# The last cross-attention batch is filled with layer norm and query and key projections of half the tokens

## The reference

```
x = x + cross_attention(layernorm(x), ctx)   # ctx: 16 x 1601 rows of 256; 16 heads of 16
x = x + self_attention(layernorm(x))         # 16 heads of 16, rotary embedding on q and k
x = x + mixture_of_experts(layernorm(x))     # 8 experts, top 2, and a shared part
x = x + linear(layernorm(x)) + mean of the projected context
x = x + self_attention(layernorm(x))         # 8 heads of 64, relative position bias
x = x + grouped_ffn(layernorm(x))
```

## Time and profile before

| | us |
|---|---|
| median of 3 runs | 1324.93 (1324.72 to 1325.19) |
| profiled execution | 1311.63 |
| span of its instructions | 1309.8 |
| TensorE busy in the span | 1186.6 (91%) |
| VectorE busy | 700.4 (53%) |
| ScalarE busy | 563.2 (43%) |
| GpSimd busy | 381.8 (29%) |

### The profile page before, as it was taken

One profiled execution on the slowest core, in us unless ns is written; L12 is line 12 of the kernel. 1 busy time (PEld: TensorE's weight loads), 2 busy tenths in 40 slices (PEclk: granted clock), 3 DMA queues, 4 the chain that ended last, 5 costly groups with the idle time before them and its releaser, 6 DMA issues. The chain is left out here.

```text
span 1309.8 us, 32326 instructions
## 1 busy us (share of the span) xinstructions
PE 1186.6 (91%) x13863; PEld 1043.7 (80%) x13863; DVE 700.4 (53%) x1111; ACT 563.2 (43%) x923; POOL 381.8 (29%) x339
## 2 busy tenths in 40 slices
PE   4799999999999999999999998787798999388799
PEld 4789989989989989989989986676577777266588
DVE  6555655655655655655655633266663221554732
ACT  4465555555555555555555552234631322121500
POOL 5632432432432432432432410044245000422000
PEclk9899999999999999999999995579989999689999
DMA  6937747747747647747647533083012121405054
GB/s 199 212 79 171 160 87 169 161 89 168 166 85 174 158 87 170 161 88 176 157 88 170 120 80 74 1 278 145 2 69 89 49 65 49 124 21 213 2 184 190
DMA packets 61732, 161.47 MB, mean 123 GB/s; under 512 B 24904, under 2 KB 38296, under 8 KB 58520
## 3 DMA queue, kind: packets, MB, share of 16 engines
q1 hardware_dynamic: 58904, 154.18, 46.6%
q0 software_dynamic: 1536, 4.20, 0.9%
q10 hardware_dynamic: 1152, 1.05, 0.2%
HBM read 70.56 MB, written 9.44 MB: 61 GB/s over the span
## 5 line engine op out<-in xcount | busy, mean ns | idle before, releaser
L366 ACT ACTIVATE xa_pt<-xa_sc 128x1024 f32<-128x1024 f32 (+1 forms) x224 | 212.4, 962 | 151.2 <-PE xa_sc L558 151.2
L412 DVE TENSOR_REDUCE xa_mx<-xa_sc 128x2 f32<-128x804 f32 x256 | 243.4, 991 | 41.5 <-PE xa_sc L542 41.5
L558 PE MATMUL xa_sc<-xa_queries,xa_keys 104*128 104x128 f32 (+1 forms) x1664 | 232.5, 285 | 2.6 <-DVE xa_queries L427 1.8
L558 PEld LDWEIGHTS xa_sc<-xa_queries,xa_keys 104*128 104x128 f32 (+1 forms) x1664 | 206.6, 195 | 21.4 <-issue 8.7
L479 PE MATMUL xa_pj<-xa_ctx_hi,xa_wk 128*128 128x400 f32 (+1 forms) x512 | 156.8, 348 | 0.9 <-DVE xa_qst L440 0.9
L479 PE MATMUL xa_pj<-xa_wv,xa_ctx_hi 128*128 128x256 f32 (+1 forms) x832 | 155.3, 286 | 0.1
L542 PE MATMUL xa_sc<-xa_keys,xa_queries 96*128 96x402 f32 x512 | 138.0, 373 | 13.1 <-DMA xa_keys<-xa_kst_hi 7.5
L569 PE MATMUL xa_op<-xa_pt,xa_values 128*32 128x64 f32 x6656 | 141.6, 228 | 7.7 <-ACT xa_pt L366 3.3
L295 POOL TENSOR_TENSOR xa_ctx_lo<-xa_raw,xa_ctx_hi 128x1600 fp32r<-128x1600 f32 (+1 forms) x32 | 115.9, 3624 | 78.0 <-DVE xa_ctx_hi L405 75.4
L300 POOL TENSOR_TENSOR xa_kst_lo<-xa_wk,xa_kst_hi 128x400 fp32r<-128x400 f32 x64 | 67.3, 1051 | 227.5 <-ACT xa_kst_hi L345 227.5
L479 PEld LDWEIGHTS xa_pj<-xa_wv,xa_ctx_hi 128*128 128x128 f32 (+1 forms) x832 | 126.1, 184 | 8.0 <-issue 6.6
(11 more groups left out here) (288 smaller groups left out, 1722.7 us busy)
## 6 DMA issues: line engine op xcount, KB each, us to landing
xa_keys<-xa_kst_hi SPq DMA_DIRECT2D x256, 200.2 KB, 6.1
xa_keys<-xa_kst_lo SPq DMA_DIRECT2D x128, 200.2 KB, 5.3
xa_raw<-in_ctxT SPq DMA_DIRECT2D x15, 1601.0 KB, 9.0
gf_w<-in_gf_w SPq DMA_DIRECT2D x16, 1024.0 KB, 7.1
moe_ex<-in_moe_ex SPq DMA_DIRECT2D x8, 1088.0 KB, 15.3
xa_queries<-xa_qst SPq DMA_DIRECT2D x96, 32.0 KB, 3.5
moe_slots_in<-in_moe_zero SPq DMA_DIRECT2D x1, 2944.0 KB, 16.2
moe_xs<-moe_slots_in SPq DMA_DIRECT2D x23, 128.0 KB, 2.2
```

What stands on the lines that cost most here:

```text
L366: nc.scalar.activation(PT[ptslot(step)][0:rows, 0:nt], SC[bank(step)][0:rows, 0:nt], ACT.Exp, scale=float(D0) ** -0.5).then_inc(ex_done, 1)
L412: nc.vector.tensor_reduce(mx[:, u // 2, 2 * (u % 2):2 * (u % 2) + 2], SC[bank(step)][:, :, 0:MXN], AX.X, ALU.max).then_inc(mx_done, 1)
L558: last = mm(SC[bank(step)][0:rows, kk, a * P:(a + 1) * P], KS[:, 2 * a + h, kt * P:kt * P + rows], QS[b % 2][:, 2 * a + h, :], start=True, ...
```

## The change

Tokens 0 to 511 (four of the eight tiles, `EARLY_TILES`) belong to batches 0 to 7, whose output steps are over long before batch 15. For them the second layer norm and the projections q, qr, k, kr are made inside `xattn`:

- first half of batch 14: "as" takes mean and variance (VectorE), the root (ScalarE), and writes the normalized tiles `ey` into the free context buffer;
- second half of batch 14: four "N" steps, two transposes each on TensorE and a copy to `lnT` on ScalarE; behind the st steps "lh" (two) and "wh" (four) split `lnT` and the weights, high parts on ScalarE, low parts on GpSimd. SyncE loads the four weights into the context buffer as soon as the last context is split;
- batch 15: eight "P" steps, four in each half, three of them between the mx steps and one ahead of mt. Each is 6 matmuls of 512 columns, a copy to SBUF on ScalarE and a multiply with cos or sin on GpSimd, every second one also an add. After each four, SyncE writes a query or key tile to DRAM (512 KB).

Layer norm 1 and the projections of `self_attention` then run over tokens 512 to 1023 alone; the values are made of all tokens. SyncE reads the early tiles back at the start of `self_attention`, ahead of the expert weights, and `projected` waits for them. The new buffers lie in the free parts of existing ones (context, key stage), which brings the waits on `kst_in` and `full["V"]`. The diff, cut to this:

```diff
@@ -35,11 +35,11 @@
-RING = ("K", "V", "Q", "E", "W")
+RING = ("K", "V", "Q", "E", "W", "N", "P")
 SCORES = ("mx", "st")
-def xattn_phase(b, h, fill, chain, late):
+def xattn_phase(b, h, fill, chain, late, between={}):
     out, fill, late = [], list(fill), dict(late)
@@ -47,6 +47,7 @@
         out.append(("mx", b, h, u))
         if fill and (u in (1, 3, 4, 6) or u >= 1 and len(fill) > 4):
             out.append(fill.pop(0))
+        out += between.get(u, [])
     out += fill + chain[:2] + [("mt", b, h, 0)] + chain[2:3]
     for g in range(7):
         out.append(("st", b, h, g))
@@ -67,12 +68,25 @@
     for b in range(B):
         queries = {2: [("Q", b // 2 + 1, 0, 0)]} if b % 2 and b + 1 < B else {}
         e = [("E", b - 1, 0, 0)] if b else []
+        if b == B - 1:
+            project = [("P", 0, 0, m) for m in range(len(EARLY))]
+            half = len(project) // 2
+            o += xattn_phase(b, 0, project[:half - 1], project[half - 1:half], {1: e})
+            o += xattn_phase(b, 1, project[half:-1], project[-1:], {})
+            continue
+        between, split_early = [{}, {}], {}
+        if b == B - 2:
+            between = [{2: [("as", 0, 0, 0)], 5: [("as", 0, 0, 1)]}, {u: [("N", n, 0, 0)] for n, u in enumerate((0, 2, 5, 7))}]
+            split_early = {1 + n: [("lh", 0, 0, n)] for n in range(CH)} | {3 + n: [("wh", 0, 0, n)] for n in range(4)}
         w = [("W", b // 2 - 1, 0, u) for u in range(2)] if b and b % 2 == 0 else []
-        o += xattn_phase(b, 0, K(b + 1, 0), V(b + 1, 0, 4), {1: e} | queries)
-        o += xattn_phase(b, 1, K(b + 1, 1) + w, V(b + 1, 4, 7), {1: split(b + 2)[:1], 4: split(b + 2)[1:]})
+        o += xattn_phase(b, 0, K(b + 1, 0), V(b + 1, 0, 4), {1: e} | queries, between[0])
+        o += xattn_phase(b, 1, K(b + 1, 1) + w, V(b + 1, 4, 7), {1: split(b + 2)[:1], 4: split(b + 2)[1:]} | split_early, between[1])
     return o + [("E", B - 1, 0, 0)] + [("W", T - 1, 0, u) for u in range(2)]
+EARLY_NAMES = ("q", "qr", "k", "kr")
+EARLY = [(n + r, ch) for n in "qk" for ch in range(CH) for r in ("", "r")]
+EARLY_TILES = T // 2
 KCOLS = [(0, 400), (400, 800), (800, 1200), (1200, NKP)]
...
@@ -253,6 +283,16 @@
                         sp.wait_ge(rows_in, 16)
                         for a in range(4):
                             sp.dma_start(*constant_rows(o_sb, slice(96 + 2 * a, 98 + 2 * a), 2 * a, 2 * a + 2)).then_inc(rows_in, 16)
+                if step == ("cv", B - 1, 0, 1):
+                    sp.wait_ge(csum_done, nth(*step) * 2)
+                    sp.wait_ge(lo_done, nth(*step))
+                    for n in EARLY_NAMES:
+                        sp.dma_start(split_by_ch(ew_raw[n]), w["sa_" + n]).then_inc(ew_in, 16)
+                if k == "P" and u in (len(EARLY) // 2 - 1, len(EARLY) - 1):
+                    j = u // (len(EARLY) // 2)
+                    sp.wait_ge(e_rot, (j + 1) * CH)
+                    sp.dma_start(early_out[j], early[j]).then_inc(early_done, 16)
                 if step in (("K", 0, 0, 3), ("K", 0, 1, 3)):
                     keys(0, h)
...
@@ -299,6 +339,28 @@
                     pool.wait_ge(khi, nth(*step))
                     nc.gpsimd.tensor_tensor(kstage[h][1][:, lo:hi], kraw[u % 2][:, 0:hi - lo],
                                             kstage[h][0][:, lo:hi].bitcast(f32), ALU.subtract).then_inc(klo, 1)
+                if k == "wh":
+                    pool.wait_ge(ewh_done, u + 1)
+                    n = EARLY_NAMES[u]
+                    nc.gpsimd.tensor_tensor(ew_lo[n], split_by_ch(ew_raw[n]), ew_hi[n].bitcast(f32), ALU.subtract).then_inc(ewl_done, 1)
+                if k == "lh":
+                    pool.wait_ge(elh_done, u + 1)
+                    nc.gpsimd.tensor_tensor(el_lo[:, u], lnT[:, u, 0:wide], el_hi[:, u].bitcast(f32), ALU.subtract).then_inc(ell_done, 1)
+                if k == "P":
+                    name, ch = EARLY[u]
+                    dst, turned = early["qk".index(name[0])][:, ch, :], name[1:] != ""
+                    by_batch = lambda a: a.rearrange("p (b s) -> p b s", s=S)
+                    table = c["sin" if turned else "cos"].unsqueeze(1).to_broadcast([P, wide // S, S])
+                    pool.wait_ge(free["P"], nth(*step))
+                    if turned:
+                        ge(pool, e_rot, u // 2)
+                    nc.gpsimd.tensor_tensor(by_batch(erot if turned else dst), by_batch(estage[u % 2]), table, ALU.mult).then_inc(e_mul, 1)
+                    if turned:
+                        pool.wait_ge(e_mul, nth(*step))
+                        nc.gpsimd.tensor_tensor(dst, dst, erot, ALU.add).then_inc(e_rot, 1)
                 if k == "E":
                     pool.wait_ge(rec_done, nth(*step))
...
@@ -357,6 +419,31 @@
                     for kk in range(nt):
                         ins = nc.scalar.activation(vdst[:, kk], vsrc[:, kk], ACT.Copy)
                     ins.then_inc(free["V"], 1)
+                elif step == ("as", 0, 0, 0):
+                    act.wait_ge(e_var, 1)
+                    nc.scalar.activation(estd[:], evar[:], ACT.Sqrt).then_inc(e_std, 1)
+                elif k == "N":
+                    act.wait_ge(full["N"], nth(*step))
+                    nc.scalar.activation(lnT[:, :, b * P:(b + 1) * P], PJ[bank(step)][:, 0:D].rearrange("p (c n) -> p c n", c=CH),
+                                         ACT.Copy).then_inc(free["N"], 1)
+                elif k == "wh":
+                    act.wait_ge(ew_in, 16 * len(EARLY_NAMES))
+                    act.wait_ge(kst_in[0], 16 * DMAS_K * B)
+                    n = EARLY_NAMES[u]
+                    nc.scalar.activation(ew_hi[n], split_by_ch(ew_raw[n]), ACT.Copy).then_inc(ewh_done, 1)
+                elif k == "lh":
+                    act.wait_ge(full["V"], nth("V", B - 1, 0, 6))
+                    act.wait_ge(free["N"], EARLY_TILES)
+                    nc.scalar.activation(el_hi[:, u], lnT[:, u, 0:wide], ACT.Copy).then_inc(elh_done, 1)
+                elif k == "P":
+                    act.wait_ge(full["P"], nth(*step))
+                    if u == 0:
+                        act.wait_ge(full["V"], nth("V", B - 1, 0, 6))
+                    ge(act, e_mul, u - 1)
+                    nc.scalar.activation(estage[u % 2], PJ[bank(step)][:, 0:wide], ACT.Copy).then_inc(free["P"], 1)
                 elif k == "st":
...
@@ -452,6 +539,20 @@
                         dve.wait_ge(free["W"], nth(*step))
                         nc.vector.bn_stats(stats[:, b], X[:, b]).then_inc(stats_done, 1)
+                elif step == ("as", 0, 0, 0):
+                    dve.wait_ge(stats_done, EARLY_TILES)
+                    for t in range(EARLY_TILES):
+                        nc.vector.bn_aggr(emv[:, t], stats[:, t]).then_inc(e_stat, 1)
+                    dve.wait_ge(e_stat, EARLY_TILES)
+                    nc.vector.tensor_scalar(evar[:], emv[:, :, 1], 1e-5, None, ALU.add).then_inc(e_var, 1)
+                elif step == ("as", 0, 0, 1):
+                    dve.wait_ge(e_std, 1)
+                    nc.vector.reciprocal(erstd[:], estd[:]).then_inc(e_stat, 1)
+                    dve.wait_ge(e_stat, EARLY_TILES + 1)
+                    dve.wait_ge(lo_done, nth("cv", B - 1, 0, 1))
+                    for t in range(EARLY_TILES):
+                        nc.vector.tensor_scalar(ey[t], X[:, t], emv[:, t, 0:1], erstd[:, t:t + 1], ALU.subtract, ALU.mult).then_inc(e_norm, 1)
                 elif k == "pv" and u == 6:
                     dve.wait_ge(pv_done, nth(*step))
...
@@ -522,6 +623,18 @@
                             last = mm(dst[:, half * P:(half + 1) * P], wq[:, ch, half * P:(half + 1) * P], lnT[:, ch, b * P:(b + 1) * P],
                                       start=ch == 0, stop=ch == CH - 1)
                     last.then_inc(full["Q"], 1)
+                elif k == "N":
+                    pe.wait_ge(e_norm, b + 1)
+                    for ch in range(CH):
+                        last = nc.tensor.transpose(dst[:, ch * P:(ch + 1) * P], ey[b][:, ch * P:(ch + 1) * P], c["ident"])
+                    last.then_inc(full["N"], 1)
+                elif k == "P":
+                    name, ch = EARLY[u]
+                    pe.wait_ge(ewl_done, EARLY_NAMES.index(name) + 1)
+                    pe.wait_ge(ell_done, CH)
+                    hs = slice(ch * P, (ch + 1) * P)
+                    split_product(dst[:, 0:wide], [(ew_hi[name][:, q, hs], ew_lo[name][:, q, hs]) for q in range(CH)],
+                                  [(el_hi[:, q, :], el_lo[:, q, :]) for q in range(CH)]).then_inc(full["P"], 1)
                 elif k == "E":
                     pe.wait_ge(o_ev, nth(*step) * 2)
...
@@ -582,6 +695,7 @@
     return W, w_in, [(W[n][:], sources[n], w_in) for n in shapes]
+LN_TILES = (T, T - EARLY_TILES, T, T, T, T)
 LN_SEMS = ("stat", "var", "std", "norm", "tr", "ev_dve", "ev_act")
@@ -594,10 +708,13 @@
     with ctx:
         sb = lambda n, s, d=f32: ctx.enter_context(nc.sbuf_tensor(f"ln{k}_{n}", s, d))
```

(44 more changed lines are left out.)

61 lines of the change are left out of this document (38 added, 23 removed).

## The result

The kernel after takes 1315.2 us (1310.0 to 1318.8), the kernel before in the same runs 1324.8 (1324.4 to 1327.2): a ratio of 0.9924, 95% interval 0.9908 to 0.9940, or 9.6 us less. The forecast was 22.7 us less. Two later measurements of the same two kernels gave 0.9930 (0.9907 to 0.9953) and 0.9908 (0.9872 to 0.9945). The profiled execution is one of 1315.2 us with a span of 1313.4.

A forecast was written before the change was run, and what follows sets the result against it. TensorE bounds the kernel through batch 14, VectorE batch 15's mx parts, TensorE at a halved clock its st/pv parts. Terms -14.9 + 3.0 - 0.5 - 10.3 = -22.7 us gave 1302.2 us; range 1298 to 1316.

The forecast's parts named there:

- Batch 15, st/pv at full clock: Score and value parts of batch 15: clock stays at 2.4 GHz, 11.1 and 10.8 us; with mx parts, 14.9 us less.
- (a): Rival: clock falls once in batch 15, in the first half's hole; +9.5 us, 1311.7 us; chance 0.17.
- (b): Rival: clock falls in both holes of batch 15; another 7.6 us over one fall, 1319.3 us; chance 0.09.
- the sum: Batch 15's halves: mx plus st/pv parts, 11.4 + 11.1 = 22.5 and 11.4 + 10.8 = 22.2 us.
- Why the clock fell in before: Batch 15's mx part: before the fall, score pairs alone, TensorE 2.97 of 4 us busy; fills make it nearly gapless.
- Batch 15, mx parts: Column maximum parts of batch 15 with four P steps each: 11.4 us per half, bounds 10.5 and 12.5.
- Batch 14: Early layer norm, transposes and splits added in batch 14's two halves: +3.0 us together.
- End of cross-attention: Output matmuls at the end of cross-attention, where the clock may have fallen again: -0.5 us, bounds -2.1 and 0.
- Layer norm 1: Layer norm after cross-attention: half its work goes, some 2 us, but no gain; values wait for the bias row's DMA.
- Self-attention: Eight of sixteen projection groups go; scores then wait for GpSimd's masked keys: -10.3 us, bounds -11.0 and -8.0.
- The last subtraction: Profiled span 1309.8 us against the runs' median 1324.9: difference taken as constant, 22.7 us subtracted from the median.

The follow-up runs named there:

- the second profile of before: The kernel before, unchanged, profiled again: median 1325.7 us, profile 1325.3 us.
- the other two: The kernel after, unchanged, run and profiled two more times: 1317.9 us and 1305.1 us.
- one pair at full clock (1311.0 against 1307.2): Unused matmuls in batch 15: kernel before, behind three maximum steps and around the mask transpose, 1311.0 us; kernel after, around the transpose only, 1307.2 us.
- another (1301.8 against 1288.4): Kernel before with 5 matmuls behind the mask transpose per half of batch 15, 1301.8 us; kernel after with each half's fourth P step moved there, 1288.4 us.

## Why the prediction was wrong

*Batch 15, st/pv at full clock: the step that failed.* I let the P steps hold the clock and took 14.9 us off; 1.3 came (0.4 against the second profile of before). The prediction named the spot, "the hole at its end: 1.76 and 0.88 us of waiting around mt", called it the weak point, and priced the loss as (a) and (b). It then weighed it wrong: 0.09 for the case that came, (b). Its reason against, that batches 13 and 14 cycle the same banks at full clock, overlooked that those have value matmuls behind mt as well, and batch 15 had its fourth P ahead of mt and nothing behind. Moving that one step behind mt gave halves of 22.43 and 21.84 us against the 22.5 and 22.2 of the sum, and a kernel 25.1 and 27.6 us under before: the term was right for the kernel with that order.

*Rival (b), 1319.3.* The clock is lost in both halves, as the windows show; the time is 4 us too slow. It took the score parts at before's 19.2 and 18.4 us. They took 17.9 and 16.9, because the clock falls 1.4 and 2.4 us after they start and not ahead of them: 2.8 of the 4 us. I had the P steps of the second half raise the clock again, after one of them at double time; in the first profile of after it was back at 818.5, and the first P's matmuls at 819.05 took 0.39 us. In the other two it came back at 821.9 and 823.2, with the first P at double time as I had it (0.63 us a matmul), and their second halves are 2 us longer.

*Why the clock fell in before.* I put it on the pauses between score pairs in the mx part. It does fall there, but the ten matmuls behind mt cure batch 15 with those pauses left as they are. Filling the mx parts was neither enough for the clock in the score parts nor needed for it.

*Batch 15, mx parts.* 11.4 us each expected; 11.64 and 11.86 measured.

*Batch 14.* +3.0 expected, +1.06 and +1.79 = +2.85 measured, with a wait of 0.57 us for VectorE ahead of mt; the halves of all runs with the change repeat it to 0.1 us. The table loads cost 1.28 us and the exponential stands 0.01 behind (750.72, 752.01): nothing of a drain behind the load shows, here as in the earlier trace rows, and none ahead of it (the copy before it ends at 750.70).

*End of cross-attention.* -0.5 expected; from the last "pv" matmul to the first value matmul it takes 17.7 us, and 17.4 and 17.5 in the two profiles of before: no gain.

*Layer norm 1.* No gain, as said: the values wait for the bias row's DMA in after too (2.88 us at 864.09).

*Self-attention.* -10.3 expected at the scores, -9.3 measured against the first profile of before and -8.9 against the second; GpSimd's masked keys release them (2.59 us at 888.48), as said. I had VectorE down for nothing there; it stands 1.1 us behind, so a faster GpSimd would have brought little more. How much of it comes through to the end is less clear: 3.8 us in one pair at full clock (1311.0 against 1307.2), 13.4 in another (1301.8 against 1288.4). In the profiles both pairs have +2.9 us in batch 14 and -10.1 at the scores, which would make 7.2. The first pair has 1.7 us more ahead of batch 14 and 2.0 more behind the start of the scores; the second has 2.3 less in batch 15 (the moved P step in place of the matmuls) and 3.5 less behind the start of the scores, though nothing was edited there. From layer norm 3's table load to the end alone the profiles differ by 4.5 us (170.0 to 174.5), so a pair of kernels says little below that; what moves them was not tried.

*The last subtraction.* "I take the difference as constant" was sound for the result and for a wrong reason: 9.8 us of the 13 are a stall in the mixture stage that some groups of runs have, for both kernels, and not something that surrounds a profile.

## What to carry to other kernels

When a stretch bound by TensorE runs at the low clock, look at what stands directly ahead of it before filling the pauses far in front: here filling one pause of 0.9 us at the start of the scores gave 6 to 9 us a half, filling the long stretch of pauses ahead of it gave under 1, and a handful of matmuls in the right place did what eight projection steps in the wrong place didn't. Put moved work where the hole is that the gain hangs on. And profile the unchanged kernel twice before building a sum on it: the profile used here lacked a stall of 10 us that the timed runs had and that has nothing to do with the change.

## What the runs showed of the hardware that I had not expected

TensorE fully busy does not mean that the clock comes back: in before the score parts keep it busy for 18 to 19 us at 0.50, while with five matmuls of 512 columns ahead of them the clock was at 1.00 for the whole part, or from less than 1 us into it. And while GpSimd's sixteen scatter DMAs are under way, ScalarE and VectorE can stand although what they wait for is done: in the second profile of before 8.5 us for ScalarE, over within 1.7 us of the last scatter's landing, and 7.8 us for VectorE, over at 1004.2, 4.7 us ahead of that landing; in some groups of runs and not in others.
